# Probabilities transposed once in float32 and split into halves on the way out of PSUM, in a group-norm attention block

## The reference

```
h    = groupnorm(x, 32 groups) * gamma + beta          # over 4 channels x 1024 pixels
q, k, v = split(w_qkv @ h + b_qkv)
attn = softmax(q^T k / sqrt(128))                      # 1024 x 1024 per image
out  = w_proj @ (attn v)^T + b_proj
return x + out
```

## Time and profile before

| | us |
|---|---|
| median of three runs | 173.06 (172.69 to 173.45) |
| span of the profiled execution | 170.8 |
| PE busy | 142.6 (83%) |
| DVE busy | 125.1 (73%) |
| ACT busy | 112.1 (66%) |
| POOL busy | 106.0 (62%) |

### The profile page before, as it was taken

The page is one execution under the profiler, slowest core; times in us unless marked ns, Lnnn a source line. Parts: engine busy times, 40 slices in busy tenths (PEclk is TensorE's granted clock), DMA queues, the critical chain, the costliest instruction groups (busy, mean ns, idle before and its releaser), DMA issues.

```text
span 170.8 us, 3310 instructions
## 1 busy us (share of the span) xinstructions
PE 142.6 (83%) x1095; PEld 83.8 (49%) x1095; DVE 125.1 (73%) x233; ACT 112.1 (66%) x152; POOL 106.0 (62%) x77
## 2 busy tenths in 40 slices
PE   0590598598599999879899998888999999999892
PEld 0540234265344656555454655454556656565481
DVE  5531739999996879949778799599675976694722
ACT  3120207899996955787978864997699699687010
POOL 7010001777989446796796459696975499669820
PEclk9997559999999999999999999999999999999999
DMA  5380000000000000100001000100010001000111
GB/s 163 83 322 0 0 0 0 2 0 4 0 0 6 0 0 4 55 9 0 4 2 61 0 0 0 61 0 0 0 61 4 0 0 61 4 2 5 57 65 61
DMA packets 2988, 4.68 MB, mean 27 GB/s; under 512 B 544, under 2 KB 1440, under 8 KB 2976
## 3 DMA queue, kind: packets, MB, share of 16 engines
q1 hardware_dynamic: 2016, 4.20, 6.8%
q10 hardware_dynamic: 832, 0.33, 0.7%
q0 software_dynamic: 128, 0.00, 0.1%
HBM read 2.43 MB, written 2.10 MB: 26 GB/s over the span
## 4 chain that ended last, share of the span: by engine, by line
PE 39%; DVE 28%; issue 17%; ACT 8%; DMA 3%; POOL 2%; ACTq 1%; DVEq 0%; POOLq 0%
DVE row_max L521 12%; PE tr L743 6%; PE scores L728 4%; PE scores L727 4%; PE scores L726 4%; DVE ptT L540 4%; ACT probs L376 3%; PE pv L761 3%; DMA gamma_c<-in_L_conv_gamma_dram 3%; PE pv L762 3%; PE pv L763 3%; DVE z L495 2%; ACT p_hi L385 2%; DVE t_lo L510 2%; DVE exp_bias L526 2%
## 5 line engine op out<-in xcount | busy, mean ns | idle before, releaser
L293 POOL TENSOR_TENSOR p_lo<-probs,p_hi 128x1024 f16<-128x1024 f32 x32 | 68.6, 2146 | 40.8 <-ACT p_hi L385 32.5
L376 ACT ACTIVATE probs<-scores,exp_bias,esc 128x1024 f32<-128x1024 f32 x32 | 38.5, 1202 | 18.1 <-DVE exp_bias L526 17.8
L521 DVE TENSOR_REDUCE row_max<-scores 128x1 f32<-128x1024 f32 x32 | 38.9, 1216 | 15.3 <-PE scores L728 15.3
L385 ACT ACTIVATE p_hi<-probs 128x1024 f16<-128x1024 f32 x32 | 33.8, 1057 | 0.8
L540 DVE COPY ptT<-tr 128x512 uint32<-128x512 uint32 x48 | 31.4, 681 | 2.6 <-PE tr L743 2.6
L726 PE MATMUL scores<-z_hi,t_hi 128*128 128x512 f16 (+1 forms) x64 | 24.7, 386 | 1.8 <-ACT probs L376 1.5
L728 PE MATMUL scores<-z_hi,t_lo 128*128 128x512 f16 (+1 forms) x64 | 24.8, 387 | 0.0
L727 PE MATMUL scores<-z_lo,t_hi 128*128 128x512 f16 (+1 forms) x64 | 24.8, 387 | 0.0
L743 PEld LDWEIGHTS tr<-ident,p_hi 128*128 128x128 f16 x256 | 16.7, 98 | 9.6 <-issue 2.6
L761 PE MATMUL pv<-ptT,v_hi 128*128 128x512 f16 x56 | 21.2, 379 | 0.0
L763 PE MATMUL pv<-ptT,v_lo 128*128 128x512 f16 x56 | 21.2, 379 | 0.0
(11 more groups left out here) (117 smaller groups left out, 220.0 us busy)
## 6 DMA issues: line engine op xcount, KB each, us to landing
out_dram<-out_sb SPq DMA_DIRECT2D x7, 256.0 KB, 2.0
x_sb<-in_x_dram SPq DMA_DIRECT2D x3, 512.0 KB, 4.8
x_sb<-in_x_dram SPq DMA_DIRECT2D x2, 256.0 KB, 3.5
out_dram<-out_sb SPq DMA_DIRECT2D x2, 128.0 KB, 1.9
wqkv_sb<-in_L_conv_w_qkv_dram ACTq DMA_DIRECT2D x1, 192.0 KB, 3.6
wp_sb<-in_L_conv_w_proj_dram ACTq DMA_DIRECT2D x1, 64.0 KB, 3.9
gamma_row<-in_L_conv_gamma_dram ACTq DMA_DIRECT2D x1, 64.0 KB, 3.9
beta_c<-in_L_conv_beta_dram POOLq DMA_DIRECT2D x1, 0.5 KB, 4.5
```

The lines of the kernel that those rows point to most:

```text
L293: nc.gpsimd.tensor_tensor(p_lo[:, s % RING], probs[:, s % RING], p_hi[:, s % RING], ALU.subtract).then_inc(plo_ready, 1)
L376: nc.scalar.activation(probs[:, s % RING], scores[:, s % 2], ACT.Exp, bias=exp_bias[:, s % 2:s % 2 + 1], scale=esc[:], accum_out=row_sum[: ...
L385: nc.scalar.activation(p_hi[:, s % RING], probs[:, s % RING], ACT.Copy).then_inc(phi_ready, 1)
L521: nc.vector.tensor_reduce(row_max[:, s % 2:s % 2 + 1], scores[:, s % 2], AX_X, ALU.max).then_inc(max_ready, 1)
```

## The change

`p_high`, `p_low` and their tiles go. PE transposes `probs` itself, in float32, eight transposes per tile in place of sixteen, four into each of two PSUM banks (a half). For each half ACT's `take_high` writes the float16 rounding to `ptT` and then DVE's `take_low` writes PSUM minus that rounding as the low half. A bank is written again when `take_low` has read it. The rounding of z for images 1 to 3 and the addition of the output bias move from ACT to POOL. The image loop is unrolled on all engines. The diff, without the declarations:

```diff
-            def z_low(b):
+            def biased_input(b):
+                if b == 0:
+                    pool.wait_ge(w_ready, 3)
+                cols = ds(b * N, N)
+                nc.gpsimd.tensor_tensor(x_sb[:, cols], x_sb[:, cols], bo[:].broadcast_to([P, N]), ALU.add
+                                        ).then_inc(xb_ready, 1)
+
+            def z_split(b):
                 for half in range(2):
+                    cols = ds(b * N + half * HALF, HALF)
+                    pool.wait_ge(z_ready, b * 2 + half + 1)
+                    nc.gpsimd.tensor_copy(z_hi[:, cols], z32[:, half * HALF:(half + 1) * HALF]).then_inc(zhi_ready, 1)
                     pool.wait_ge(zhi_ready, b * 2 + half + 1)
-                    cols = ds(b * N + half * HALF, HALF)
                     nc.gpsimd.tensor_tensor(z_lo[:, cols], z32[:, half * HALF:(half + 1) * HALF], z_hi[:, cols],
                                             ALU.subtract).then_inc(zlo_ready, 1)
-
-            def p_low(b, s):
-                g = b * TILES + s
-                pool.wait_ge(exp_ready, g + 1)
-                pool.wait_ge(phi_ready, g + 1)
-
-                wait(pool, tr_lo, g - RING + 1)
-                nc.gpsimd.tensor_tensor(p_lo[:, s % RING], probs[:, s % RING], p_hi[:, s % RING],
-                                        ALU.subtract).then_inc(plo_ready, 1)
...
-                        z_low(b + 1)
-                    if cur:
-                        p_low(b, s)
+                        z_split(b + 1)
+                    if cur and s == 3:
+                        biased_input(b)
...
-                wait(act, plo_ready, g - RING + 1)
+                wait(act, tr_ready, 2 * (g - RING + 1))
...
-            def p_high(b, s):
-                g = b * TILES + s
-                act.wait_ge(exp_ready, g + 1)
-
-                wait(act, tr_hi, g - RING + 1)
-                nc.scalar.activation(p_hi[:, s % RING], probs[:, s % RING], ACT.Copy).then_inc(phi_ready, 1)
-
             def take_high(b, i):
 
+                g = b * TILES + i
                 c, j = divmod(i, CT)
                 if j == 0:
 
                     wait(act, pv_ready, (b - 1) * CHUNKS + c + 1)
-                act.wait_ge(tr_hi, b * TILES + i + 1)
-                nc.scalar.activation(ptT[:, c, 0, :, j * P:(j + 1) * P],
-                                     tr[:, 0].rearrange("p (k q) -> p k q", k=TILES), ACT.Copy
-                                     ).then_inc(ptT_hi_even, 1)
+                for half in range(2):
+                    act.wait_ge(tr_ready, 2 * g + half + 1)
+                    nc.scalar.activation(ptT[:, c, 0, half * CT:(half + 1) * CT, j * P:(j + 1) * P],
+                                         tr[:, half].rearrange("p (k q) -> p k q", k=CT), ACT.Copy
+                                         ).then_inc(ptT_hi, 1)
...
-                    if nxt and s == 5:
-                        z_high(b + 1)
                     if nxt and s == 7:
                         t_high(b + 1, 0)
-                    if prev and s == 1:
-                        take_high(b - 1, s + TILES - T_LAG)
-                    if cur and s >= T_LAG and (s - T_LAG) % 2 == 0:
-                        take_high(b, s - T_LAG)
                     if cur:
                         exponentials(b, s)
                     if cur and s in (1, 5):
                         v_high(b, s // CT)
-                    if cur:
-                        p_high(b, s)
-                    if cur and s == 3:
-                        if not prev:
-
-                            act.wait_ge(w_ready, 3)
-
-                        nc.scalar.activation(x_sb[:, ds(b * N, N)], x_sb[:, ds(b * N, N)], ACT.Identity,
-                                             bias=bo[:]).then_inc(xb_ready, 1)
-
-            images(act, body)
+                    if prev and s < T_LAG:
+                        take_high(b - 1, s + TILES - T_LAG)
+                    if cur and s >= T_LAG:
+                        take_high(b, s - T_LAG)
+
+            images(body)
...
-            def take_transposes(b, i):
+            def take_low(b, i):
                 g = b * TILES + i
                 c, j = divmod(i, CT)
-                h = b * CHUNKS + c
-                if j == 0:
-
-                    wait(dve, pv_ready, h - CHUNKS + 1)
-                for part, (ready, taken) in enumerate(((tr_hi, ptT_hi_odd), (tr_lo, ptT_lo))):
-                    if part == 0 and i % 2 == 0:
-                        continue
-                    dve.wait_ge(ready, g + 1)
-                    nc.vector.tensor_copy(
-                        ptT[:, c, part, :, j * P:(j + 1) * P].bitcast(U32),
-                        tr[:, part].bitcast(U32).rearrange("p (k q) -> p k q", k=TILES)).then_inc(taken, 1)
+                for half in range(2):
+                    dve.wait_ge(ptT_hi, 2 * g + half + 1)
+                    ks, qs = slice(half * CT, (half + 1) * CT), slice(j * P, (j + 1) * P)
+                    nc.vector.tensor_tensor(ptT[:, c, 1, ks, qs], tr[:, half].rearrange("p (k q) -> p k q", k=CT),
+                                            ptT[:, c, 0, ks, qs], ALU.subtract).then_inc(ptT_lo, 1)
...
-                        take_transposes(b - 1, s + TILES - T_LAG)
+                        take_low(b - 1, s + TILES - T_LAG)
                     if cur and s >= T_LAG:
-                        take_transposes(b, s - T_LAG)
+                        take_low(b, s - T_LAG)
...
             def transposes(b, i):
                 g = b * TILES + i
-                for part, (src, ready, done) in enumerate(((p_hi, phi_ready, tr_hi), (p_lo, plo_ready, tr_lo))):
-                    pe.wait_ge(ready, g + 1)
-
-                    if part == 1:
-                        wait(pe, ptT_lo, g)
-                    elif i % 2:
-                        pe.wait_ge(ptT_hi_even, b * (TILES // 2) + (i + 1) // 2)
-                    else:
-                        wait(pe, ptT_hi_odd, b * (TILES // 2) + i // 2)
-                    for k in range(TILES):
-                        last = nc.tensor.transpose(tr[:, part, k * P:(k + 1) * P],
-                                                   src[:, i % RING, k * P:(k + 1) * P], ident16[:])
-                    last.then_inc(done, 1)
+                pe.wait_ge(exp_ready, g + 1)
+                for half in range(2):
+
+                    wait(pe, ptT_lo, 2 * (g - 1) + half + 1)
+                    for k in range(CT):
+                        src = (half * CT + k) * P
+                        last = nc.tensor.transpose(tr[:, half, k * P:(k + 1) * P],
+                                                   probs[:, i % RING, src:src + P], ident32[:])
+                    last.then_inc(tr_ready, 1)
...
-                    pe.wait_ge(ptT_hi_even, b * (TILES // 2) + (c + 1) * CT // 2)
-                    pe.wait_ge(ptT_hi_odd, b * (TILES // 2) + (c + 1) * CT // 2)
-                    pe.wait_ge(ptT_lo, b * TILES + (c + 1) * CT)
+                    pe.wait_ge(ptT_lo, 2 * (b * TILES + (c + 1) * CT))
                     pe.wait_ge(attn_ready, h + 1)
```

More of the change, by code:

```diff
@@ L127, in attention_block @@
         probs = sb("probs", [P, RING, N])
-        p_hi = sb("p_hi", [P, RING, N], F16)
-        p_lo = sb("p_lo", [P, RING, N], F16)
         row_sum = sb("row_sum", [P, CHUNKS, CT])
@@ L141, in attention_block @@
         scores = pb("scores", [P, 2, N])
-        tr = pb("tr", [P, 2, N], F16)
+        tr = pb("tr", [P, 2, HALF])
         pv = pb("pv", [P, HALF])
@@ L204, in attention_block @@
         exp_ready = sem("exp_ready")
[L205 to L210, removed]
+        tr_ready = sem("tr_ready")
+        ptT_hi = sem("ptT_hi")
         ptT_lo = sem("ptT_lo")
@@ L227, in wait, with images @@
                 eng.wait_ge(s, value)
[L229 to L236, removed]
+        def images(body):
+            for b in range(B + 1):
+                body(b, prev=b > 0, cur=b < B, nxt=b < B - 1)
         block = ctx.enter_context(nc.Block())
@@ L336, in body @@
                         diagonals(b, 0)
-            images(pool, body)
+            images(body)
         @block.scalar
@@ L347, in _, with z_high_first @@
             act.dma_start(gamma_c[:], col(gamma)).then_inc(w_loaded, 16)
-            def z_high(b):
+            def z_high_first():
                 for half in range(2):
-                    act.wait_ge(z_ready, b * 2 + half + 1)
-                    nc.scalar.activation(z_hi[:, ds(b * N + half * HALF, HALF)],
+                    act.wait_ge(z_ready, half + 1)
+                    nc.scalar.activation(z_hi[:, half * HALF:(half + 1) * HALF],
                                          z32[:, half * HALF:(half + 1) * HALF], ACT.Copy).then_inc(zhi_ready, 1)
@@ L409, in _ @@
             nc.scalar.activation(wpT[:], scores[:, 1, 0:P], ACT.Copy).then_inc(wpT_ready, 1)
-            z_high(0)
+            z_high_first()
             t_high(0, 0)
@@ L684, in body @@
                         normalise(b + 1)
-            images(dve, body)
```

(7 more changed lines are left out.)

## The result

The changed kernel takes 205.96 us (median of 4 runs, 204.92 to 206.69), the kernel before 173.03 us (172.69 to 173.45): ratio 1.190, interval 1.185 to 1.194. The prediction was 204.5 us, slower. The profiled execution of the changed kernel took 206.3 us with a span of 204.4.

A forecast was written before the change was run, and what follows sets the result against it. The bound was taken to be a closed wait between VectorE and ScalarE, 4.51 us per tile. Last reduction at 181.3, drain 12.2 and rest 8.7 gave span 202.2; with 2.3 to the median, 204.5 us, range 195 to 216.

The forecast's parts named there:

- The bound: TensorE sets the pace before; after the change its 4.4 us per tile is hidden beside 5.5 us of circle.
- circle: Per tile, VectorE's reduction, ScalarE's exponential and half copy, VectorE's subtractions wait in turn: 1.49, 1.20, 0.62, 1.20; 4.51 us.
- The middle images: Each middle image: eight turns of 4.51 us plus 8.4 us of other work and stall, 44.5 us.
- The stall: In middle images GpSimd's residual add meets VectorE's mean_g after scale_output: 1.0 us more, between 0 and 1.1.
- The last reduction: Start of VectorE's last reduction: 32.5 + 126.3 + 22.5 = 181.3 us, now 151.5.
- The drain: Last reduction to first matmul of pv_last: three tiles of transposes, copy, subtraction, then inverse sums and diagonals; 12.2 us.
- The float32 transposes: On TensorE, eight per tile at 0.15 us each, 1.2 us, 0.3 more than now; ends 0.055 and 0.39.
- Not slower: Rival: the circle does not bite, TensorE stays the bound; 0 to 14 us off, 159 to 173 us; 6 in 100.
- Transposes at 0.39 us: Rival: float32 transposes as slow as the early passes, TensorE needs 6.3 us per tile; 226 us; 6 in 100.
- The clock falls: Rival: TensorE's clock drops to 1.2 GHz in the gaps; 231 us for one image, some 300 for all; 4 in 100.
- my signs of being wrong: Reductions 4.2 us apart or less, subtraction not waiting for ScalarE, or the clock row dropping in the main part.
- The range: Circle's own range 197 to 214 us, from -6 to +8 and stalls 0 to 4; put forward 195 to 216.

The follow-up runs named there:

- e1: Changed kernel with ScalarE's half copies moved ahead of the exponential; 165.64 us, ratio 0.957 to the kernel before.
- e2: Changed kernel with one whole copy and one whole subtraction of 1024 columns per tile instead of two halves of each; 218.09 us, ratio 1.260.
- e3: Changed kernel with every float32 transpose issued twice, 256 more; 207.11 us, ratio 1.197.
- e4: Changed kernel with VectorE's group mean of the next image moved ahead of the output scaling in middle images; 204.18 us, ratio 1.180.
- e7: Changed kernel with ScalarE's half copies ahead of the exponentials and VectorE's group mean ahead of the output scaling; 164.90 us, ratio 0.952.
- e8: e7 with every float32 transpose issued twice, 256 more; 185.46 us, ratio 1.070.
- e5: Kernel before with only its loop over the images unrolled; 171.02 us, ratio 0.987.
- e6: Unrolled kernel before with ScalarE's copy of the transposed high halves moved behind the exponentials of its turn; 178.55 us, ratio 1.033.

## Why the prediction was right, and where it was off

**The bound and the circle: right.** Predicted 4.51 us per turn, measured 4.52, each of its four pieces within 0.02 us. e1 opens it (-40.3 us), e2 lengthens it, e3 shows that TensorE's work is not what is late.

**The middle images: right in the sum.** 44.5 us predicted; 44.40 both times. The stall fell on var_in, not on mean_g as I wrote: GpSimd's addition starts as soon as attn has ended (119.30 us), and there var_in is next (119.32), while in the kernel before GpSimd's subtraction happened to start one instruction later. Its size, 1.0 us, held (e4).

**The last reduction: right.** 181.3 predicted, 181.39 measured:

```profile
181.39 1.22 DVE L496 TENSOR_REDUCE row_max<-scores 128x1 f32<-128x1024 f32 x1
```

On the way image 0's tile 3 started at 33.2 rather than 32.5 and the others gave it back, so this agreement has some luck in it. Most of that 0.7 lies ahead of the main part: the first reduction started at 25.75 us, in the kernel before at 25.1, and in the runs above anywhere from 25.05 to 26.12.

**The drain: mis-sized by 0.5 us, and 1.6 us for the clock.** 12.2 us predicted from there to the first matmul of pv_last, 14.4 measured (195.75; the earlier trace rows have 10.6). This 2.2 us is the whole miss of the span, 202.2 for 204.4. TensorE's rows:

```profile
185.54 1.16 PE L708 MATMUL tr<-ident,probs 128*128 128x128 f32 x8 [2.51 <-DVE ptT L510]
186.54 0.38 PE L724 MATMUL pv<-ptT,v_hi 128*128 128x512 f16 x1
186.75 0.59 PE L725 MATMUL pv<-ptT,v_hi 128*128 128x512 f16 x1
...
189.70 1.29 PE L708 MATMUL tr<-ident,probs 128*128 128x128 f32 x8
```

I had the chain of three tiles as transposes, copy, subtraction, and left out eight matmuls that stand on TensorE between the transposes of two of these tiles. Seven of them, from 186.75 to 189.70 us, ran 0.42 us apart, at half clock, where 0.22 is usual: 1.4 us. Then ScalarE's r_sb copy (0.60 us) stood ahead of the half copies. e4 has the same instructions in the drain, and there the clock stayed up behind the same pause:

```profile
184.80 1.16 PE L708 MATMUL tr<-ident,probs 128*128 128x128 f32 x8 [2.51 <-DVE ptT L510]
...
187.10 0.38 PE L749 MATMUL misc<-diag_hi,ones 128*128 128x512 f16 x1
```

Its drain took 12.73 us (180.65 to 193.38). So 1.6 of the 2.2 us are the lower clock, which I had priced only for whole images, and 0.5 us are left for what the chain left out. The four runs of the changed kernel agree: the one with the highest mean clock, 0.972, is the fastest at 204.92 us, the one with the lowest, 0.933, the slowest at 206.69.

**The float32 transposes: mis-sized, without effect.** I took 0.15 us; they measure 0.109. In the kernel before sixteen float16 ones at 0.055 made 0.88 us per tile, now eight make 0.87: the change saves TensorE nothing there. I had set the rule of the Trainium skill ("TensorE: Matmul & The Clock Gate", Terms, float32 four times faster in transpose mode) at the low end of 0.055; that was my reading, and e7 and e8 rule it out. The page does not say four times faster than what; if a plain float32 matmul is meant, no run here has one of 128 columns at full clock beside the transposes.

**The unrolling: left out.** I gave it no term. It was worth 2.2 us to the kernel before (e5); what it is worth in the changed kernel no run shows.

**The rivals.** "Not slower" asked that the subtraction never wait; it has 32 waits, 54.1 us in all. "Transposes at 0.39 us" falls with 0.109. "The clock falls" came in a small way: 0.96 in each middle image, less than 0.1 us in their turns, 1.6 us in the drain. Its stretch of 4.03 busy us in 6.00 at 1.00 was therefore poor evidence against it. A drop of the clock row in the main part was even one of my signs of being wrong, and the row did drop, to 0.7 in two slices, while the circle held: the sign was too strict.

**The range: added up loosely.** -6 to +8 us and 0 to 4 us of stalls around 204.5 give 198.5 to 216.5, not 197 to 214. The range put forward, 195 to 216, does not hang on it.

## What to carry to other kernels

Lighter work on two engines (here ScalarE and GpSimd) does not help if one instruction newly needs what another engine issues late: follow one turn through both engines' orders, and where the wait comes back to where it began, the time of a turn is the sum around that circle. The remedy is then the order, not the work: here the copy ahead of the exponential turned 206 us into 165.6. Whether an engine is the bound is told by doubling its work in both versions (1.2 us against 20.6 us).

## What the runs showed of the hardware

**The clock after a pause.** In the changed kernel, TensorE's rows after an idle stretch of 2.39 us:

```profile
124.72 1.55 PE L708 MATMUL tr<-ident,probs 128*128 128x128 f32 x8 [2.39 <-DVE ptT L510]
126.07 0.63 PE L724 MATMUL pv<-ptT,v_hi 128*128 128x512 f16 x1
...
128.91 0.38 PE L750 MATMUL misc<-diag_lo,ones 128*128 128x512 f16 x1
```

Matmuls of 0.63 us, at 1.2 GHz, until 128.6 us, then 0.38 us, at 2.4 GHz, again. In e6 a pause of 2.09 us goes with the same, behind float16 transposes:

```profile
73.10 0.61 PE L740 MATMUL tr<-ident,p_hi 128*128 128x128 f16 x8 [2.09 <-ACT ptT L391]
...
74.51 0.63 PE L760 MATMUL pv<-ptT,v_lo 128*128 128x512 f16 x1
```

In e5, e7 and e8, whose middle images have no pause as long as 1.2 us, the clock is 1.00 in all of them, in e8 with sixteen float32 transposes per tile. So the dips went with pauses, not with float32 or with transposes. But a pause does not settle it. The changed kernel kept 0.38 behind a pause of 2.79 us (47.79 us), e4 behind one of 2.51 (184.80, above), e6 behind its second one of 2.09 (110.40). And e4 has matmuls of 0.63 us behind a pause of only 1.21 us:

```profile
53.02 1.47 PE L708 MATMUL tr<-ident,probs 128*128 128x128 f32 x8 [1.21 <-DVE ptT L510]
54.28 0.63 PE L724 MATMUL pv<-ptT,v_hi 128*128 128x512 f16 x1
```

What decides between them these runs do not show, and it differs from run to run of one kernel: the mean clock of the changed kernel's four runs goes from 0.933 to 0.972.

**VectorE beside GpSimd.** var_in, one element per partition from SBUF operands, lasted 1.26 us beside a GpSimd addition and 0.22 without (e4). The pair z lasted 2.81 us beside a GpSimd subtraction and 1.00 without (e5).

**A float32 transpose of 128x128** goes at 0.109 us at 2.4 GHz, twice the 0.055 of float16.
